# Two attentions: the heads' output brought to features by DMA, compact sums, and products of ones at the start of each

## The chip, the cores and the metric

One core of a Trainium2 chip runs the kernel. Its engines are TensorE (PE in the profile; PEld its weight loads), VectorE (DVE), ScalarE (ACT), GpSimd (POOL) and SyncE (SP, which here issues every DMA). The metric is the device time of one execution in microseconds (us), taken as the median of several.

## What is computed

Two sequences of 1024 tokens with 512 features go through six steps. Each step takes a layer norm of x and adds its result to x.

```python
x = x + 0.5 * ffn(layernorm(x))             # W + lora_B @ lora_A, scaled by column
x = x + attention0(layernorm(x))            # 32 query heads of 16, 8 key heads, rotary
x = x + 0.5 * ffn(layernorm(x))
x = x + 0.5 * experts(layernorm(x))         # base + top 2 of 8 experts of rank 16
x = x + attention1(layernorm(x))            # 8 heads of 32, scale 1
x = x + 0.5 * experts(layernorm(x))
# attention: softmax(q @ k.T * scale, causal) @ v, heads side by side, @ w_o.T + b_o
```

All of it is held to float32 accuracy. So a matrix product is made of three passes (high x high, high x low, low x high), with operands split into a high and a low part.

## The kernel before

Each sequence b runs three chains of dense stages and, between them, two attentions: chain 0 (`FFN_A`, `QKV0`), attention `QKV0`, chain 1 (`WO0`, `FFN_B`, `MOE_A`, `QKV1`), attention `QKV1`, chain 2 (`WO1`, `MOE_B`). A dense stage works on eight tiles of 128 tokens, one in each tick of its chain. In a tick TensorE transposes ("turns") the tile of one stage (`turn_x`), ScalarE casts it to its high part (`copy_turned`), VectorE takes the low part (`turned_lo`), and TensorE multiplies the tile turned a tick earlier (`product`). VectorE adds the product to x (`epilogue`), GpSimd adds biases (`bias_x`, L1484) and takes the low parts of the next stage's weights (`split_chunk`, L1466) behind ScalarE's casts of them.

An attention runs in units: 8 units of 4 heads in the first (`A0`), 4 units of 2 heads in the second (`A1`). A unit has 12 steps (c, j): c is the half of the 1024 queries, j the block of 128 keys. Steps 0 to 3 belong to half 0, steps 4 to 11 to half 1; in steps 0 to 3 and 8 to 11 the block lies on the diagonal. In each step TensorE makes the scores transposed, keys by queries (L977, L983), ScalarE takes their exponentials (L1431), GpSimd masks those on the diagonal (L1542), and two or three steps later TensorE multiplies by the values (L999). The values carry a column of ones, so the sum of the exponentials comes out as one more row of each head. Scores, exponentials and values have banks 0 to 3 and 6 of PSUM.

The exponentials need a shift, minus the maximum of each query's scores, which enters the scores as two more rows of the queries. These maxima are worked out about one unit ahead, in a ring of three PSUM banks. `plan_ring` writes the order of the ring's items out beforehand, at three slots in each step, and TensorE (`ring_item`) and VectorE (`ring_read`) both walk through it. There are three kinds of items:

- "max": TensorE makes scores in the other orientation (L871) and VectorE takes maxima by row (L1204 on the diagonal, L1208 off it).
- "shift": a half's shifts (from L1247 to L1253) are transposed (L876), copied (L1217), and SyncE writes them into the query rows by small DMAs (`load_shifts`, L606).
- "norm": when the values of half c of a unit are complete, ScalarE copies them out of PSUM (`heads_raw`, L1418). Four transposes (L881) bring them to tokens by features, VectorE takes the reciprocals of the sums (L1227) and multiplies (L1232) into `features`.

An item takes its bank when the item three places ahead has been read. The ring runs ahead of the scores from the start: the first items stand in chain 0 or 1, among the products of `QKV0` or `QKV1`, the next (`ring_first`) by themselves, and in the first steps of unit 0 more of them stand in each slot than later (`wanted`). At the end of an attention, `WO0` or `WO1` turns the eight tiles of `features` as any other stage does.

SyncE's queue holds all DMAs in one order, with waits between them. In the first attention each unit has the shifts of the next unit, the queries of the unit three ahead, and in two units a stage's weights.

## Time and profile before

| | us |
|---|---|
| median of 3 runs | 1364.15 (1360.6 to 1367.84) |
| profiled execution | 1344.81 |
| its span, first to last instruction | 1343.1 |
| TensorE busy | 1205.7 (90%) |
| VectorE busy | 953.5 (71%) |
| ScalarE busy | 671.2 (50%) |
| GpSimd busy | 375.2 (28%) |

The page gives busy time by engine, the span in 40 slices of 33.6 us, the DMA queues, the chain of waits that ended last, and groups of instructions by line. In the slices each digit is a share in tenths. The clock that TensorE was granted is given in the same way, 9 being nine tenths or more of full speed. The two sequences take about half of the span each. The attentions lie at about 108 to 358, 527 to 619, 771 to 1021 and 1186 to 1278 us.

### The profile page before, as it was taken

The numbers are of one execution on the slowest core, as the hardware profiler recorded it, in microseconds if no ns is written. First come the engines' busy times: TensorE is split into PE (matmuls) and PEld (weight loads), VectorE is DVE, ScalarE is ACT, GpSimd is POOL, SyncE is SP. The second block draws the span as 40 slices with busy tenths as digits, with TensorE's granted clock in tenths as the row PEclk, the third lists the DMA queues.
The fourth block names the chain that finished last, engine by engine and source line by source line (L and its number), as shares of the span: only waits on it lengthen the run. The fifth ranks groups of instructions, "written<-read, shape, count | busy, mean of one in ns | idle before, by whom it ended". The sixth has DMA issues, their size and how long they took to land.

```text
span 1343.1 us, 21792 instructions
## 1 busy us (share of the span) xinstructions
PE 1205.7 (90%) x6800; PEld 753.2 (56%) x6800; DVE 953.5 (71%) x2990; ACT 671.2 (50%) x1023; POOL 375.2 (28%) x505
## 2 busy tenths in 40 slices
PE   4998999999899877998879999999988988879988
PEld 1875444443388865444868744444435887744368
DVE  5889889898166676653659798999962667576365
ACT  2621666666655452544436036666665554435542
POOL 0431411122254400114614323122213542002162
PEclk9996899999999997999979858999999999869999
DMA  8374411220010020100140742112200100120001
GB/s 317 120 196 87 125 29 26 57 65 3 1 49 1 1 47 19 55 2 0 63 175 23 189 130 70 26 26 57 66 2 0 50 1 17 32 72 2 1 8 56
DMA packets 37285, 76.20 MB, mean 57 GB/s; under 512 B 5084, under 2 KB 6620, under 8 KB 37036
## 3 DMA queue, kind: packets, MB, share of 16 engines
q1 hardware_dynamic: 37176, 74.82, 19.2%
q8 instruction: 60, 0.98, 0.3%
q14 instruction: 49, 0.40, 0.1%
HBM read 48.98 MB, written 27.08 MB: 57 GB/s over the span
## 4 chain that ended last, share of the span: by engine, by line
PE 64%; DVE 19%; issue 5%; POOL 5%; ACT 5%; DMA 1%; DVEq 0%; SPq 0%; ACTq 0%; POOLq 0%
PE bank L999 16%; PE bank L871 12%; PE bank L779 5%; PE bank L780 5%; PE bank L781 5%; DVE maxes L1208 5%; PE bank L983 4%; PE bank L977 3%; DVE unused L1204 3%; PE bank L765 3%; DVE ops L1152 3%; PE bank L881 2%; POOL x L1484 2%; POOL w_odd L1466 2%; ACT ops L1356 2%
## 5 line engine op out<-in xcount | busy, mean ns | idle before, releaser
L1431 ACT ACTIVATE probs<-bank 128x1024 f32<-128x1024 f32 (+3 forms) x416 | 367.9, 911 | 320.4 <-PE bank L983 220.3
L871 PE MATMUL bank<-ops 48*128 48x512 f32 (+3 forms) x960 | 321.8, 436 | 34.5 <-DVE maxes L1204 17.2
L1204 DVE CUSTOM_DVE_ANT_0 unused<-bank,causal 128x128 bf16<-128x128 f32 (+3 forms) x640 | 279.5, 486 | 47.7 <-PE bank L871 44.1
L1542 POOL TENSOR_SCALAR_AFFINE_SELECT probs<-probs 128x256 f32<-128x256 f32 (+1 forms) x256 | 118.8, 464 | 640.3 <-ACT probs L1431 640.0
L871 PEld LDWEIGHTS bank<-ops 48*128 48x128 f32 (+1 forms) x960 | 163.0, 206 | 218.9 <-DVE maxes L1204 96.0
L999 PE MATMUL bank<-probs,v_mem 128*17 128x512 f32 (+6 forms) x1920 | 252.2, 517 | 6.1 <-ACT heads_raw L1418 5.6
L1208 DVE TENSOR_REDUCE maxes<-bank 128x1 f32<-128x512 f32 x320 | 207.4, 684 | 40.7 <-PE bank L871 39.2
L983 PE MATMUL bank<-ops 50*128 50x512 f32 (+2 forms) x640 | 175.9, 448 | 5.0 <-ACT probs L1431 4.8
L779 PE MATMUL bank<-ops,xT 128*128 128x512 f32 (+1 forms) x288 | 116.2, 403 | 19.6 <-DVE x L1068 11.6
L983 PEld LDWEIGHTS bank<-ops 50*128 50x128 f32 x640 | 86.6, 197 | 57.9 <-ACT probs L1431 29.5
L1473 POOL TENSOR_TENSOR rstd<-var_eps,minus_half 128x1 f32<-128x1 f32 x96 | 52.7, 549 | 215.1 <-DVE var_eps L1046 214.5
L1315 ACT CAST xT<-bank 128x512 fp32r<-128x512 f32 (+1 forms) x96 | 52.6, 548 | 118.0 <-PE bank L765 117.9
L1055 DVE TENSOR_TENSOR xT<-bank,xT 128x512 fp32r<-128x512 f32 (+1 forms) x96 | 61.5, 643 | 67.5 <-ACT xT L1315 67.1
L780 PE MATMUL bank<-ops,xT 128*128 128x512 f32 (+1 forms) x288 | 105.5, 366 | 0.0
L781 PE MATMUL bank<-ops,xT 128*128 128x512 f32 (+1 forms) x288 | 105.5, 366 | 0.0
L999 PEld LDWEIGHTS bank<-probs,v_mem 128*17 128x17 f32 (+1 forms) x1920 | 40.9, 99 | 77.1 <-issue 52.0
L1374 ACT ACTIVATE probs<-x,ln_bias,rstd 128x512 f32<-128x512 f32 x96 | 78.3, 816 | 3.2
L779 PE MATMUL bank<-w_odd,xT 128*128 128x324 f32 (+1 forms) x192 | 72.8, 379 | 5.8 <-DVE x L1068 2.7
L1227 DVE RECIPROCAL inv_sum<-bank 128x16 f32<-128x16 f32 (+1 forms) x48 | 11.3, 234 | 92.6 <-PE bank L881 92.6
L779 PEld LDWEIGHTS bank<-ops,xT 128*128 128x128 f32 x288 | 56.4, 196 | 31.2 <-issue 21.4
L765 PE MATMUL bank<-identf,probs 128*128 128x128 f32 x384 | 57.8, 280 | 16.0 <-ACT probs L1374 16.0
L1042 DVE BATCH_NORM_STATS2 stats<-x 128x6 f32<-128x512 f32 x96 | 65.8, 686 | 3.7 <-DMA x<-x_dram 3.3
(117 smaller groups left out, 1965.5 us busy)
## 6 DMA issues: line engine op xcount, KB each, us to landing
query_rows_dram<-ops SPq DMA_DIRECT2D x48, 256.0 KB, 3.8
ops<-query_rows_dram SPq DMA_DIRECT2D x64, 192.0 KB, 4.4
w_odd<-staging_wqkv SPq DMA_DIRECT2D x4, 1536.0 KB, 7.3
x<-x_dram SPq DMA_DIRECT2D x16, 256.0 KB, 6.1
ops<-ops SPq DMA_DIRECT2D x16, 256.0 KB, 3.0
out_dram<-x SPq DMA_DIRECT2D x16, 256.0 KB, 2.0
staging_wqkv<-wqkv_dram SPq DMA_DIRECT2D x2, 1536.0 KB, 15.8
key_rows_dram<-ops SPq DMA_DIRECT2D x24, 128.0 KB
```

The source lines that it names most:

```text
L765: last = nc.tensor.transpose(turn[n % 2][:, k * P:(k + 1) * P], src[:, k * P:(k + 1) * P], identf[:])
L779: mm(dst, x_hi[:, k, :], hi[:, k, :], start=(k == 0), stop=False)
L780: mm(dst, x_hi[:, k, :], lo[:, k, :], start=False, stop=False)
L781: last = mm(dst, x_lo[:, k, :], hi[:, k, :], start=False, stop=(k == kc - 1 and not lora))
L871: last = mm(dst[:, h * w:(h + 1) * w], queries(a, u)[rows, t // 4, hi, t % 4 * P:(t % 4 + 1) * P], keys(a, u, hi)[rows, HALF * kp:HALF * k ...
L983: last = mm(dst, keys(a, u, 0)[rows, block], queries(a, u)[rows, c, heads_of[0]:heads_of[-1] + 1, columns], start=True, stop=True)
L999: last = mm(heads[a.head_rows * h:a.head_rows * h + a.dim + 1, q0 - HALF * c:HALF], v[:, j, a.kv_head(u, r, i), :], probs[:, e % 6, n, fir ...
L1204: V.tensor_tensor_reduce(unused[:, masked % 3, 0:w], part, causal[:, HALF - w:], 1.0, NEG, ALU.add, ALU.max, dst).then_inc(s["max_done"].s ...
L1208: V.tensor_reduce(dst, part, AX.X, ALU.max).then_inc(s["max_done"].sem, 1)
L1374: A.activation(xn[n % XN_SLOTS], x[:, t, :], ACT.Identity, bias=ln_bias[:, i, :], scale=rstd[:, i, :]).then_inc(xn_ready.sem, 1)
L1431: A.activation(probs[:, e % 6, :, 0:cols], scores[:, 2 * (e % 2):2 * (e % 2) + 2, 0:cols], ACT.Exp, scale=a.scale).then_inc(s["exp"].sem, 1)
L1542: G.affine_select(out=p, in_=p, compare_op=ALU.is_ge, fill=0.0, base=0, pattern=pattern, channel_multiplier=-1).then_inc(s["masked"].sem, 1)
```

## The change

The "norm" items leave the ring, and with them the transposes L881, the reciprocals L1227 and the multiplications L1232. `heads_raw` keeps the heads as rows and queries as columns, and this is also what the output product wants of its operand, features by tokens. So the change never turns them:

- SyncE writes a chunk of `heads_raw` to DRAM (`load_heads`). It reads the heads' rows back, packed into 64 partitions for a unit, and the rows of sums as 128 partitions of 16 (8 in the second attention).
- For each pair of units and half, VectorE takes the reciprocals of the compact sums (`inverse_sums`). SyncE stores them and loads them back spread over the rows of each head (`spread_inverse`).
- GpSimd multiplies, casts to the high part and subtracts for the low part (`heads_out`), ahead of step 4 of a later unit. For the last pair VectorE does this (`last_heads`), half 0 at the end of the attention, half 1 in tick 5 of the chain that follows.
- `WO0` and `WO1` take these parts (`heads_T`) as their operands. Their turns, ScalarE's copies of them and VectorE's low parts are gone. The products of tiles 0 to 3 wait for half 0, those of tiles 4 to 7 for half 1.
- ScalarE's copy of a chunk waits for the dump of the chunk two back, where it waited for a ring item.
- The parts lie where `MOE_A`'s weights were loaded early. These weights are now loaded after `WO0` and split at tiles 4 to 7 of `FFN_B`, not 2 to 5. `xT` has moved to the end of `ops`.
- TensorE multiplies a 128x128 block of ones by a 128x512 one, in bfloat16, ahead of every second "max" item between the chain's part of the ring and step 3 of the first unit. The result goes to the item's own bank, which the item then overwrites. There are 20 of these in each first attention and 7 in each second.

```diff
-                if slot == 0:
-                    for c in range(2):
-                        e = s - self.lag - 2 - self.last_step[c]
-                        if e >= 0 and e % ns == 0 and e // ns < self.units:
-                            dst.append(("norm", e // ns, c))
         self.ring = self.ring_first + [x for step in self.ring_at for slot in step for x in slot]
         self.ring_len = len(self.ring)
-        self.norm_at = [i for i, item in enumerate(self.ring) if item[0] == "norm"]
...
+        def heads_T(a, part, k):
+            first = ((4096, 5120, 6144, 7168), (8192, 9216, 21504, 14336)) if a is A0 else ((1024, 3072), (4096, 5120))
+            return ops_flat[:, first[part][k]:first[part][k] + SEQ]
...
+            def load_heads(b, st, u, c):
+                a, s = ATT[st], qs[st]
+                lanes, n = slice(64 * (u % 2), 64 * (u % 2) + 64), a.unit_heads * HALF // P
+                sp.wait_ge(s["raw"].sem, s["raw"].at(b, 2 * u + c + 1))
+                wait(sp, s["staged"][c], b, 32 * u)
+                sp.dma_start(raw_rows[c], heads_raw[:, c, :]).then_inc(s["dumped"][c].sem, 16)
+                sp.wait_ge(s["dumped"][c].sem, s["dumped"][c].at(b, 16 * (u + 1)))
+                if u == 0 and c == 0 and a.rope:
+                    sp.wait_ge(s["lo"].sem, s["lo"].at(b, 6))
+                if u > 3:
+                    sp.wait_ge(s["out"].sem, s["out"].at(b, 3 * (2 * (u // 2 - 2) + c) + 1))
+                rows = raw_rows[c].rearrange("(h r) s -> h r s", r=a.head_rows)
+                sp.dma_start(head_in[lanes, u // 2 % 2, c, :], rows[:, 0:a.dim, :]).then_inc(s["staged"][c].sem, 16)
+                sp.dma_start(sums[:, c, u % 2, 0:n], rows[:, a.dim, :].rearrange("h (l x) -> h l x", x=n)
+                             ).then_inc(s["staged"][c].sem, 16)
+            def spread_inverse(b, st, k, c):
+                a, s = ATT[st], qs[st]
+                n = a.unit_heads * HALF // P
+                flat = inverse_rows[c, 0:2 * n * P]
+                sp.wait_ge(s["inverse"].sem, s["inverse"].at(b, 2 * k + c + 1))
+                wait(sp, s["spread"][c], b, 16 * k)
+                sp.dma_start(flat.rearrange("(u l x) -> l u x", u=2, x=n), sums[:, c, :, 0:n]).then_inc(s["inverse_stored"].sem, 16)
+                sp.wait_ge(s["inverse_stored"].sem, s["inverse_stored"].at(b, 16 * (2 * k + c + 1)))
+                if k > 0:
+                    sp.wait_ge(s["out"].sem, s["out"].at(b, 3 * (2 * (k - 1) + c) + 1))
+                rows = flat.rearrange("(h s) -> h s", s=HALF).unsqueeze(1)
+                sp.dma_start(head_inv[:, c, :], rows.to_broadcast([2 * a.unit_heads, a.dim, HALF])).then_inc(s["spread"][c].sem, 16)
...
+                    if u % 2 == 0 and u > 0:
+                        spread_inverse(b, QKV0, u // 2 - 1, 1)
+                    load_heads(b, QKV0, u, 0)
+                    if u % 2:
+                        spread_inverse(b, QKV0, u // 2, 0)
+                    if u + 1 < a.units:
                         load_shifts(b, QKV0, u + 1, 1)
                     if u + 3 < a.units:
 
                         sp.wait_ge(s["scored"].sem, s["scored"].at(b, (u + 1) * a.unit_events))
                         load_queries(b, u + 3, 0)
                         load_queries(b, u + 3, 1)
-                    if u in (3, 4):
-                        load_weights(b, FFN_B if u == 3 else MOE_A)
+                    if u == 3:
+                        load_weights(b, FFN_B)
+                    load_heads(b, QKV0, u, 1)
+                spread_inverse(b, QKV0, a.units // 2 - 1, 1)
...
+                load_weights(b, MOE_A)
...
                 n = product_no(st, t)
-                pe.wait_ge(xT_ready.sem, xT_ready.at(b, TURN_NO[st, t] + 1))
+                if st in WO_ATT:
+                    a, s = WO_ATT[st], qs[QKV0 if st == WO0 else QKV1]
+                    pe.wait_ge(s["out"].sem, s["out"].at(b, 3 * (a.units - 2)))
+                    pe.wait_ge(s["last"].sem, s["last"].at(b, 3 * (t // 4 + 1)))
+                else:
+                    pe.wait_ge(xT_ready.sem, xT_ready.at(b, TURN_NO[st, t] + 1))
                 wait(pe, x_new, b, n - 1)
...
                     operands_ready(b, st, u, t)
+                    if max(a.begun.values()) <= i < len(a.ring_first) + sum(len(slot) for step in a.ring_at[:3] for slot in step) and i % 2:
+                        mm(dst, ones_b[:, 0:P], ones_b[:, :], start=True, stop=True)
...
-                else:
-                    c = 2 * u + n
-                    pe.wait_ge(s["raw"].sem, s["raw"].at(b, c + 1))
-                    for j in range(4):
-                        last = nc.tensor.transpose(dst[:, j * P:(j + 1) * P],
-                                                   heads_raw[:, c % 2, j * P:(j + 1) * P], identf[:])
...
+                    if c > 0 and i == 3:
+                        inverse_sums(b, QKV0 if c == 1 else QKV1, (A0 if c == 1 else A1).units // 2 - 1, 1)
+                    if c > 0 and i == 5:
+                        last_heads(b, QKV0 if c == 1 else QKV1, 1)
...
-                    V.reciprocal(inv_sum[:, 0:4 * nh].unsqueeze(2), blocks[:, :, d:d + 1]).then_inc(s["inv"].sem, 1)
-                    dve.wait_ge(s["inv"].sem, s["inv"].at(b, c + 1))
-                    width = a.q_feats
-                    dst = features[:, :].rearrange("p (t f) -> p t f", f=D)[
-                        :, 4 * n:4 * n + 4, u * nh * d:(u + 1) * nh * d].rearrange("p t (h d) -> p t h d", h=nh)
-                    V.tensor_tensor(dst, src.rearrange("p (t h r) -> p t h r", t=4, h=nh)[:, :, :, 0:d],
-                                    inv_sum[:, 0:4 * nh].rearrange("p (t h) -> p t h", t=4).unsqueeze(3)
-                                    .to_broadcast([P, 4, nh, d]), ALU.mult).then_inc(s["normed"].sem, 1)
+            def inverse_sums(b, st, k, c):
+                a, s = ATT[st], qs[st]
+                part = sums[:, c, :, 0:a.unit_heads * HALF // P]
+                dve.wait_ge(s["staged"][c].sem, s["staged"][c].at(b, 32 * (2 * k + 2)))
+                V.reciprocal(part, part).then_inc(s["inverse"].sem, 1)
+            def last_heads(b, st, c):
+                a, s = ATT[st], qs[st]
+                k = a.units // 2 - 1
+                hi, lo = (heads_T(a, part, k)[:, HALF * c:HALF * (c + 1)] for part in range(2))
+                dve.wait_ge(s["spread"][c].sem, s["spread"][c].at(b, 16 * (k + 1)))
+                dve.wait_ge(s["out"].sem, s["out"].at(b, 3 * (2 * (k - 1) + c + 1)))
+                V.tensor_tensor(head_out[:, c, :], head_in[:, k % 2, c, :], head_inv[:, c, :], ALU.mult).then_inc(s["last"].sem, 1)
+                dve.wait_ge(s["last"].sem, s["last"].at(b, 3 * c + 1))
+                V.tensor_copy(hi, head_out[:, c, :]).then_inc(s["last"].sem, 1)
+                dve.wait_ge(s["last"].sem, s["last"].at(b, 3 * c + 2))
+                V.tensor_tensor(lo, head_out[:, c, :], hi.bitcast(F32), ALU.subtract).then_inc(s["last"].sem, 1)
 
             def attention(b, st):
-                for i in range(max(ATT[st].begun.values()), ATT[st].ring_len):
-                    ring_read(b, st, i)
+                a = ATT[st]
+                ring_no = max(a.begun.values())
+                for g, step in [(-1, [a.ring_first])] + list(enumerate(a.ring_at)):
+                    upto = len(a.ring_first) + sum(len(slot) for before in a.ring_at[:g + 1] for slot in before)
+                    for i in range(ring_no, upto):
+                        ring_read(b, st, i)
+                    ring_no = upto
+                    u, k_ = divmod(g, len(a.steps))
+                    if u % 2 == 0 and 0 < u < a.units and k_ == 6:
+                        inverse_sums(b, st, u // 2 - 1, 1)
+                    if u % 2 == 1 and u < a.units and k_ == 10:
+                        inverse_sums(b, st, u // 2, 0)
+                last_heads(b, st, 0)
...
-                                act.wait_ge(s["ring_full"].sem, s["ring_full"].at(b, a.norm_at[ch - 2] + 1))
+                                act.wait_ge(s["dumped"][c].sem, s["dumped"][c].at(b, 16 * (ch // 2)))
...
+                        first = 4 if nst == MOE_A else 2
+                        if nb < BATCH and nst not in WO_ATT and first <= t < first + chunks_of[nst]:
+                            split_chunk(nb, nst, t - first)
...
+            def heads_out(b, st, k, c):
+                a, s = ATT[st], qs[st]
+                n = 3 * (2 * k + c)
+                hi, lo = (heads_T(a, part, k)[:, HALF * c:HALF * (c + 1)] for part in range(2))
+                pool.wait_ge(s["staged"][c].sem, s["staged"][c].at(b, 32 * (2 * k + 2)))
+                pool.wait_ge(s["spread"][c].sem, s["spread"][c].at(b, 16 * (k + 1)))
+                G.tensor_tensor(head_out[:, c, :], head_in[:, k % 2, c, :], head_inv[:, c, :], ALU.mult).then_inc(s["out"].sem, 1)
+                pool.wait_ge(s["out"].sem, s["out"].at(b, n + 1))
+                G.tensor_copy(hi, head_out[:, c, :]).then_inc(s["out"].sem, 1)
+                pool.wait_ge(s["out"].sem, s["out"].at(b, n + 2))
+                G.tensor_tensor(lo, head_out[:, c, :], hi.bitcast(F32), ALU.subtract).then_inc(s["out"].sem, 1)
...
+                    if u > 1 and k_ == 4:
+                        heads_out(b, st, u // 2 - 1, u % 2)
```

SyncE's queue in the first attention, around units 1 to 3. `shiftT` are the shifts, `query_rows` the queries. Before:

```order
45 L606 DMA ops<-shiftT 1x8x128 x8
46 L639 DMA ops<-query_rows_dram 48x2x512 x4
47 L606 DMA ops<-shiftT 1x8x128 x8
48 L639 DMA ops<-query_rows_dram 48x2x512 x4
49 L606 DMA ops<-shiftT 1x8x128 x8
50 L639 DMA ops<-query_rows_dram 48x2x512 x4
```

With the change, from the queries of one unit to those of the next but one (`raw_rows` holds a dumped chunk, `inverse_rows` the inverses):

```order
61 L674 DMA ops<-query_rows_dram 48x2x512 x4
62 L619 DMA raw_rows_dram<-heads_raw 128x512
63 L626 DMA features<-raw_rows_dram 64x1x512
64 L627 DMA sums<-raw_rows_dram 128x1x16
65 L609 DMA ops<-shiftT 1x8x128 x4
66 L637 DMA inverse_rows_dram<-sums 128x2x16
67 L642 DMA features<-inverse_rows_dram 128x1x512
68 L619 DMA raw_rows_dram<-heads_raw 128x512
69 L626 DMA features<-raw_rows_dram 64x1x512
70 L627 DMA sums<-raw_rows_dram 128x1x16
71 L609 DMA ops<-shiftT 1x8x128 x4
72 L674 DMA ops<-query_rows_dram 48x2x512 x4
```

The second half's four shift loads stand behind a dump, its two loads, a store and a spreading load.

TensorE at the start of the first attention, behind the last product of `QKV0`. Before:

```order
292 L871 MATMUL bank<-ops 128x512 x3
293 L876 MATMUL bank<-identf,shifts 32x128
294 L871 MATMUL bank<-ops 128x512
295 L871 MATMUL bank<-ops 128x128 x4
296 L871 MATMUL bank<-ops 128x512 x4
297 L871 MATMUL bank<-ops 128x256 x4
298 L871 MATMUL bank<-ops 128x512 x3
299 L983 MATMUL bank<-ops 128x512 x2
```

With the change (L928 is the product of ones, L931 the maxima, L936 the shifts):

```order
292 L931 MATMUL bank<-ops 128x512
293 L928 MATMUL bank<-ones_b 128x512
294 L931 MATMUL bank<-ops 128x512 x2
295 L936 MATMUL bank<-identf,shifts 32x128
296 L931 MATMUL bank<-ops 128x512
297 L928 MATMUL bank<-ones_b 128x512
298 L931 MATMUL bank<-ops 128x128 x4
299 L928 MATMUL bank<-ones_b 128x512
300 L931 MATMUL bank<-ops 128x512 x2
301 L928 MATMUL bank<-ones_b 128x512
302 L931 MATMUL bank<-ops 128x512 x2
303 L928 MATMUL bank<-ones_b 128x512
```

Between the maxima stand seven products of ones ahead of the first scores, and thirteen more behind.

GpSimd in the first attention, masks only. Before:

```order
75 L1542 AFFINE_SELECT probs<-probs 128x2x128 x4
76 L1542 AFFINE_SELECT probs<-probs 128x4x128
77 L1542 AFFINE_SELECT probs<-probs 128x2x256
78 L1542 AFFINE_SELECT probs<-probs 128x2x128 x4
79 L1542 AFFINE_SELECT probs<-probs 128x4x128
```

With the change (L1633 are the masks):

```order
85 L1633 AFFINE_SELECT probs<-probs 128x4x128
86 L1633 AFFINE_SELECT probs<-probs 128x2x256
87 L1605 TENSOR_TENSOR features<-features 128x512
88 L1607 CAST ops<-features 128x512
89 L1609 TENSOR_TENSOR ops<-features,ops 128x512
90 L1633 AFFINE_SELECT probs<-probs 128x2x128 x4
91 L1633 AFFINE_SELECT probs<-probs 128x4x128
```

Three operations on 128x512 elements have come between the masks of steps 3 and 8.

## Rows read from the trace of the kernel before

**Rows 1.** The page: busy time of each engine; TensorE's granted clock by slice.

```profile
PE 1205.7 (90%) x6800; PEld 753.2 (56%) x6800; DVE 953.5 (71%) x2990; ACT 671.2 (50%) x1023; POOL 375.2 (28%) x505
...
PEclk9996899999999997999979858999999999869999
```

**Rows 2.** Busy time by stretch: two units of the first attention, its last the second.

```profile
core 0: us, PE busy (x) PEld busy (x) DVE busy (x) ACT busy (x) POOL busy (x), PEclk, DMA share, GB/s
...
202.30:230.60 28.30, 27.55 (x197) 11.73 (x194) 26.32 (x92) 19.02 (x24) 5.80 (x12) 1.00 0.14 30
...
317.80:346.20 28.40, 22.84 (x168) 8.49 (x165) 14.55 (x42) 18.54 (x24) 5.80 (x12) 1.00 0.01 2
```

**Rows 3.** Chain of waits by line: two units of either attention, first the first's.

```profile
by line: PE bank L999 31.3%; PE bank L871 28.5%; DVE maxes L1208 13.3%; PE bank L983 11.7%; issue 5.1%; DVE unused L1204 4.5%; PE bank L881 4.2%; DVE maxes L1204 1.6%; PE bank L876 0.7%; DVEq L1202 0.1%
...
by line: PE bank L999 41.8%; PE bank L871 24.9%; PE bank L977 23.6%; PE bank L881 4.0%; ACT heads_raw L1418 2.7%; ACT probs L1431 1.4%; PE bank L876 1.0%; issue 0.7%
```

**Rows 4.** Groups of instructions by line: busy, mean ns of one, idle before.

```profile
L881 PE MATMUL bank<-identf,heads_raw 128*128 128x128 f32 x192 | 31.5, 288 | 5.5 <-ACT heads_raw L1418 3.1 <-DVE maxes L1208 2.3
L1484 POOL TENSOR_TENSOR x<-x,bo 128x512 f32<-128x512 f32 x32 | 41.0, 1286 | 0.0
...
L1232 DVE TENSOR_TENSOR features<-bank,inv_sum 128x256 f32<-128x256 f32 x48 | 20.4, 424 | 1.7
...
L1227 DVE RECIPROCAL inv_sum<-bank 128x16 f32<-128x16 f32 (+1 forms) x48 | 11.3, 234 | 92.6 <-PE bank L881 92.6
```

**Rows 5.** Timeline (start, length, instruction, idle before it): GpSimd, and VectorE beside it.

```profile
210.59 0.41 POOL L1542 TENSOR_SCALAR_AFFINE_SELECT probs<-probs 128x256 f32<-128x256 f32 x1 [13.58 <-ACT probs L1431]
...
134.61 2.35 POOL L1497 TENSOR_TENSOR ops<-features,ops 128x1024 fp32r<-128x1024 f32 x1
134.71 2.29 DVE L1253 SCALAR_TENSOR_TENSOR shifts<-maxes,shifts 128x16 fp32r<-128x16 f32 x1
```

**Rows 6.** Timeline: one unit's second shift rows, and the scores that want them.

```profile
188.49 0.18 DVE L1253 SCALAR_TENSOR_TENSOR shifts<-maxes,shifts 128x16 fp32r<-128x16 f32 x1
...
190.45 2.63 SPq L606 DMA_DIRECT2D ops<-shiftT  x4
...
197.18 0.50 PE L983 MATMUL bank<-ops 50*128 50x512 f32 x2
```

**Rows 7.** DMA issues (count, size, us to landing); timeline: VectorE's wait for a load.

```profile
out_dram<-x SPq DMA_DIRECT2D x16, 256.0 KB, 2.0
...
689.54 0.69 DVE L1042 BATCH_NORM_STATS2 stats<-x 128x6 f32<-128x512 f32 x1 [3.27 <-DMA x<-x_dram]
```

**Rows 8.** Timeline: from the first attention into its output product, first sequence.

```profile
346.12 0.62 ACT L1418 COPY heads_raw<-bank 128x512 f32<-128x512 f32 x1
...
362.10 0.71 PE L779 MATMUL bank<-w_odd,xT 128*128 128x512 f32 x1 [0.96 <-DVE xT L1055]
...
386.14 0.48 PE L779 MATMUL bank<-w_odd,xT 128*128 128x512 f32 x1
...
388.77 0.39 PE L781 MATMUL bank<-w_odd,xT 128*128 128x512 f32 x1
```

**Rows 9.** Timeline: from the second attention into its output product, first sequence.

```profile
609.01 0.58 ACT L1418 COPY heads_raw<-bank 128x512 f32<-128x512 f32 x1
...
621.99 0.79 PE L779 MATMUL bank<-ops,xT 128*128 128x512 f32 x1 [0.70 <-DVE xT L1055]
...
626.38 1.59 POOL L1466 TENSOR_TENSOR w_odd<-w_odd 128x648 fp32r<-128x648 f32 x1 [6.83 <-ACT w_odd L1324]
...
640.22 0.39 PE L781 MATMUL bank<-ops,xT 128*128 128x512 f32 x1
```

**Rows 10.** Busy time by stretch: starts of three attentions (columns as in rows 2).

```profile
112.00:148.00 36.00, 34.11 (x127) 17.33 (x126) 31.48 (x103) 13.59 (x15) 7.58 (x8) 0.53 0.59 163
764.00:816.00 52.00, 49.13 (x187) 27.20 (x187) 43.38 (x138) 15.64 (x17) 10.09 (x10) 0.51 0.42 116
528.00:540.00 12.00, 11.83 (x33) 6.89 (x33) 8.98 (x35) 3.84 (x5) 1.63 (x4) 0.51 0.30 96
```

116 lines of the change are left out of this document (62 added, 54 removed).

## The prediction

> **What bounds the kernel now.** I read the page's busy shares and clock line first, then the two attentions unit by unit, then the chain of waits. TensorE is busy for 90% of the span at a mean clock that falls in a few slices [rows 1]; the low slices are those in which an attention starts. In steady units of the first attention (28.3 us each) TensorE is busy 27.55 us and VectorE 26.32 us, both near the full length [rows 2]. The chain of waits passes back and forth between TensorE's products and VectorE's maxima, and the transposes of the heads (L881) hold 4.2% of it there, 4.0% in the second attention [rows 3]. Work that leaves both engines therefore shortens a unit. In the last unit (row 317.80) VectorE is down to 14.55 us and TensorE to 22.84: the exponentials set the pace, and the same work taken out gains nothing.
>
> **The change, part by part.** The sum is made against the profiled execution's own 1344.81 us and then scaled to the median, 1364.15; the two lie 1.4% apart.
>
> *The transposes of the heads leave the ring.* 48 groups of four go, with 48 reciprocals (0.23 us) and 48 multiplications (0.42 us) on VectorE [rows 4]. In the first attention the chain gives L881 4.2% of 57.7 us, so 2.4 us for four groups, 0.60 each. VectorE loses 0.65 us a group and gets back one reciprocal per two chunks, so it does not become the new bound. 13 groups per sequence lie before the tail: 13 x 0.60 x 2 = 15.6 us. In the second, 4.0% of 43.8 us is 1.75 us for four groups, 0.44 each; 5.5 groups per sequence lie before its tail: 4.8 us. Ends: half of this if VectorE's order keeps TensorE waiting anyway, all of it and 2 us more if the waits around the groups go too.
>
> *GpSimd gets three operations of 128x512 for each pair of units and half.* The nearest row is the bias addition, 1.29 us [rows 4], so up to 3.9 us in a unit. They stand ahead of steps 4 to 7, in which GpSimd has nothing to mask: it sits idle for 13.58 us there [rows 5]. Cost zero, hidden in that gap; beyond 13 us they would delay the masks and with them the values. One collision is possible: a VectorE operation with two inputs in SBUF took 2.29 us in place of 0.18 while GpSimd ran a 2.35 us one [rows 5]. The Trainium skill (SBUF — State Buffer, "SBUF: two separate sides") says that VectorE with two SBUF inputs and GpSimd take a shared pair of ports as an exclusive lock for a whole instruction; the trace agrees. The maxima read PSUM and at most one SBUF input; the two-input operations of a half come just ahead of step 4 and at the end of the unit, so I take nothing for it in the sum and keep it as a rival.
>
> *SyncE's queue.* Per chunk it now issues a dump, waits for it, issues two loads; per pair a store of the inverses, a wait, and a spreading load. The load of the second half's shift rows stands behind that in odd units, and TensorE's scores of step 4 wait for these rows. Before: last maximum worked up at 188.49, four shift loads issued 190.45 to 193.08, wanted at 197.18 [rows 6]. After: the reciprocal runs two short maxima later, about 189.5; store landed 191.8 (2.2 us, between a 256 KB store's 2.0 and a load's 3.27 [rows 7]); the spreading load issued by 192.4; shift loads by 195.1, landed 2 us later at 197.1. So no slack is left: 0 to 2 us late in each of six such places, I take 0.5: +3 us. In the second attention only two loads are issued and the store is over earlier; nothing.
>
> *The turn to the output product.* Before, the last chunk is transposed, divided, transposed again, cast and split ahead of the first product. After, the operand's parts come by the DMA chain. Its price: three large transfers at 2.7 us (2.0 to 3.27), a small one at 2.2, a second issue 0.6 (2.63 us for four [rows 6]), the reciprocal 0.25, three VectorE operations of 512 columns at 0.7, handoffs 0.6: 13.9 us, ends 11 and 17. First attention: the first half's chunk is copied at 346.12 to 346.74, so its parts are ready at 360.6 and the product starts at 360.8, where it was 362.10 [rows 8]. The tiles also lose their transposes; a product's matmuls stand 0.24 us apart (eleven gaps from 386.14 to 388.77), and eight tiles from 362.10 to 389.0 hold seven turns of 0.35: 2.5 us. The second half's chain starts its reciprocal behind the first tile's update (about 365.9) and ends at 373.5, when tile 3 ends: no wait. End 385.2 for 389.0: -3.8 us, twice -7.6. Ends: 0 and -5 each.
>
> Second attention: copied by 609.59, ready at 623.5, where the product started at 621.99 [rows 9]. Its tiles are half as long: first tile done 626.4, update 627.1, then 7.7 us for reciprocal, store, spreading and split: 634.8. Four tiles of six matmuls and the next stage's turns end at 641.3, later if the clock fell in the wait. Before: 640.5. GpSimd no longer holds this stretch: it had waited 6.83 us for a cast that stood behind the turned tile's copy (626.38), and that copy is gone, so it is ahead from now on. I take +1.5 us, twice +3. Ends -2 and +5 each.
>
> *Weights of the expert stage* load after the output product and are split two tiles later, a stage ahead of their use: zero.
>
> *The ones products.* 20 in each first attention, 7 in each second. At full clock one costs 0.24 us, at half clock 0.48. In the starts of the attentions the granted clock is 0.53, 0.51 and 0.51, about the 1.2 GHz level, and VectorE idles 4.5, 8.6 and 3.0 us in them [rows 10]; at the steady share (2.0 of 28.3) it would be 2.5, 3.6 and 0.8. If the products keep the clock at 2.4 GHz, the gain is 2.0 + 5.0 + 2.2 + 2.2 (the second sequence's like the first's) = 11 us. If they don't, 13 of 20 stand among scores and are paid at 0.48, and all 7: 2 x (6.2 + 3.4) = 19 us. What speaks for: the products use all rows and TensorE sits waiting for VectorE here. Against: during 112 to 148 TensorE was busy 34.11 of 36 us and the clock still stayed low. Between these ends I take 0. The Trainium skill (TensorE: Matmul & The Clock Gate, "What's actually happening") states that the throttled clock is the default and activity releases it; by that alone the first end would hold, and the sum would be 11 us lower. The row of 112 to 148 does not fit it without more.
>
> **Sum.** -15.6 - 4.8 + 3 - 7.6 + 3 + 0 = -22 us: 1322.8 for 1344.81, a factor 0.9836, and 1342 us for the median.
>
> **The rivals.**
> 1. The clock holds through the starts: 11 us more, 1331. For it: idle TensorE rows at the start of an attention; against: the busy stretch above. 0.20.
> 2. The clock does not hold (that part does not do what it says) and the products are paid: +19, 1361. 0.14.
> 3. The shared ports: one two-input VectorE operation per unit falls into a GpSimd one and loses 0.9 us (between 0 and 1.29) in the units with such work: 16 x 0.9 = +14, 1356. Against it is the order of the operations. 0.05.
> 4. Slower: the transfers of the sums and inverses in pieces of 64 bytes (32 in the second attention) land late. Each chunk's sums and each pair's inverses go so. At d us more for each, six shift waits grow by d, the turns by about 2d (four of them, of which the later ones twice). At d = 3: 6 x 3 + 2 x 6 + 2 x 6 = 42, so +20 against the old kernel, scaled 1384. It decides from d = 1.6 on, where the gain is gone. The shift rows, 512 bytes a piece, land in about 2 us, which speaks against it. The Trainium skill (DMA: Bandwidth & Descriptors, "Why small descriptors are slow") says that small pieces are slow for HBM; no run here shows these sizes, and the amount is only 8 to 16 KB. 0.09.
>
> **How the numbers follow.** The forecast, 1334 to 1350, has 0.52. Faster than before by over 0.5% (about what a measurement can tell, so below 1357.3) hold the forecast, rival 1, and parts of 2 and 3: 0.78. Within 0.5%: the rest of 2 and 3 and the mild end of 4, 0.13. Slower: 0.09. The range 1325 to 1362 takes in the forecast, most of rival 1, rivals 2 and 3, and leaves rival 4 and the far end of 1 out.
>
> **What would show it.** Units of the first attention of 27.1 us in place of 28.3; no wait of the scores for shift rows above 1 us; the first output product at about 361 and 623.5 less what was gained ahead of it; GpSimd's three operations ended ahead of the masks of step 8; the granted clock in the four starts near 1.0 (rival 1) or still 0.5 with fewer idle VectorE microseconds (rival 2). The prediction is wrong if units keep 28 us although L881 is gone, or if the turns take over 17 us from the copy.

## The result, and the profile after

The change makes the kernel slower. Its median is 1374.65 us (1368.35 to 1378.83, 6 runs) against 1362.33 for the kernel before (1356.39 to 1367.84, 6 runs): a ratio of 1.0104, with an interval of 1.0059 to 1.0149. On another chip the same pair gave 1.0118 (1.0065 to 1.0172, `change_again` below). The ratios, here and below, leave out executions more than 1.5% above the fastest of the same kernel. I had forecast 1342 us, a ratio of 0.984.

The profiled execution of the change has a span of 1366.3 us, that of the kernel before 1343.1. The profiled one of before was short: 1344.81 us, below all six timed runs. So the two traces differ by 23 us where the medians differ by 12, and I read pieces from them, not the total.

First the page of the change: the busy times, and TensorE's granted clock by slice. Against [rows 1] TensorE has 11.6 us less work and VectorE 16 us less, although 27.1 us of products of ones came in, and yet the span is longer. Work was taken out; waiting came in. The mean granted clock of the span is lower too, 0.910 for 0.928.

```profile
PE 1194.1 (87%) x6560; PEld 728.6 (53%) x6566; DVE 937.5 (69%) x2911; ACT 655.9 (48%) x991; POOL 427.8 (31%) x553
...
PEclk8996799799999998997989958899999999989889
```

**At full clock the units did what they were to do.** Busy time by stretch: two units of the first attention with the change, of which [rows 2] show the one before.

```profile
core 0: us, PE busy (x) PEld busy (x) DVE busy (x) ACT busy (x) POOL busy (x), PEclk, DMA share, GB/s
198.28:225.36 27.08, 26.38 (x188) 10.78 (x188) 25.30 (x89) 18.86 (x23) 8.93 (x15) 1.00 0.31 73
252.83:285.28 32.45, 31.95 (x188) 13.12 (x190) 25.66 (x89) 19.09 (x22) 8.91 (x15) 0.75 0.34 94
```

The first unit takes 27.08 us where it took 28.30, and VectorE 25.30 where it was busy for 26.32. The second takes 32.45 us with the same number of matmuls, because the clock was at 0.75 of full speed. One such fall costs 5 us, four units' gain. They come in the kernel before as well, at other places and of other lengths: from the first copy of the heads to the first half's last one its first attentions have a mean clock of 0.97 and 0.97, those of the change 0.94 and 0.92. What brings them no run here separates.

**The turn to the output product is where most of the time went.** (Turn is here the passage from an attention to its output product, not a transpose.) The timeline around the second attention's last copies, first sequence: SyncE, then VectorE, then TensorE (start, length, instruction, idle before it and its cause). The rows of the kernel before are [rows 9].

```profile
609.48 0.33 SPq L619 DMA_DIRECT2D raw_rows_dram<-heads_raw  x1
611.86 0.51 SPq L626 DMA_DIRECT2D features<-raw_rows_dram  x1
612.41 0.48 SPq L627 DMA_DIRECT2D sums<-raw_rows_dram  x1
617.80 0.37 SPq L637 DMA_DIRECT2D inverse_rows_dram<-sums  x1
619.37 0.56 SPq L642 DMA_DIRECT2D features<-inverse_rows_dram  x1
...
617.52 0.25 DVE L1282 RECIPROCAL sums<-sums 128x16 f32<-128x16 f32 x1 [20.22 <-DMA sums<-raw_rows_dram]
624.89 1.99 DVE L1291 TENSOR_TENSOR features<-features 128x512 f32<-128x512 f32 x1 [7.12 <-DMA features<-inverse_rows_dram]
626.92 1.37 DVE L1293 CAST ops<-features 128x512 fp32r<-128x512 f32 x1
628.32 0.69 DVE L1295 TENSOR_TENSOR ops<-features,ops 128x512 fp32r<-128x512 f32 x1
...
629.12 0.77 PE L830 MATMUL bank<-ops 128*128 128x512 f32 x1 [11.22 <-issue]
...
641.72 0.77 PE L830 MATMUL bank<-ops 128*128 128x512 f32 x1 [4.39 <-issue]
```

The copy of the first half starts at 608.88. The dump is issued at 609.48 and has landed when the loads are issued, at 611.86. Then nothing happens on VectorE until 617.52: the reciprocal waits for both loads. The spreading load, issued at 619.37, lands at 624.89. VectorE's three operations take 1.99, 1.37 and 0.69 us. TensorE starts at 629.12, after 11.22 us of idling: 20.2 us behind the copy's start, where it was 13.0 in the kernel before. At tile 4 it idles once more, 4.39 us at 641.72, for the second half's chain.

The same stretch by busy time, with the clock and the share of the 16 DMA engines:

```profile
618.60:624.60 6.00, 0.00 (x0) 0.00 (x0) 0.00 (x0) 2.56 (x5) 5.64 (x5) 0.68 0.27 84
624.60:629.10 4.50, 0.00 (x0) 0.01 (x1) 4.05 (x3) 0.00 (x0) 3.40 (x3) 0.50 0.08 20
629.10:634.10 5.00, 4.99 (x12) 3.94 (x13) 0.85 (x2) 0.00 (x0) 0.00 (x0) 0.50 0.08 17
```

In the wait the clock has fallen, to a mean of 0.68 and then 0.50, and the product's first 5 us are paid at 0.50. The first attention's turn is less bad: 18.5 us from copy to product for 16.0 before, and tile 4 doesn't wait.

**The products of ones were paid.** Timeline of TensorE near the start of the first attention, first sequence, and their group over the whole execution (busy, mean ns, idle before):

```profile
113.25 0.39 PE L928 MATMUL bank<-ones_b 128*128 128x512 bf16 x1
...
120.98 0.61 PE L928 MATMUL bank<-ones_b 128*128 128x512 bf16 x1
...
L928 PE MATMUL bank<-ones_b 128*128 128x512 bf16 x48 | 27.1, 564 | 8.7 <-DVE maxes L1266 8.5
...
124.00:136.00 12.00, 11.53 (x34) 5.39 (x34) 10.41 (x41) 1.62 (x2) 0.98 (x3) 0.50 0.13 24
```

They last 0.61 us each once the clock is down, and it comes down as it did without them: over 124 to 136 us the granted clock is 0.50. The first copy of the heads stands at 150.72 us, in the kernel before at 143.24. Of the 54, the weight loads show all and the matmul records 48, so the 27.1 us are those of 48.

**Minor terms.** Scores waited for shift rows seldom, 0.6 us in all in the first attentions and 6.8 us in six places of the second (kernel before: 0.8). GpSimd's three operations waited 0.5 us for their data and lie in the gap they were put in.

```profile
PEld bank L1030 <- DMA ops<-shiftT: 6.8, 6, 2.0
...
PEld bank L1036 <- DMA ops<-shiftT: 0.6, 1, 0.6
```

### The profile page after: what moved, and what is told of

It is laid out like the page before. It is cut to its first block, busy times and chain, and to the rows that moved or that the text cites. A ratio compares the mean times of both kernels' runs of the same rounds, so it can differ in the third digit from the quotient of the medians.

```text
span 1366.3 us, 21474 instructions
## 1 busy us (share of the span) xinstructions
PE 1194.1 (87%) x6560; PEld 728.6 (53%) x6566; DVE 937.5 (69%) x2911; ACT 655.9 (48%) x991; POOL 427.8 (31%) x553
## 4 chain that ended last, share of the span: by engine, by line
PE 63%; DVE 17%; issue 7%; ACT 5%; POOL 4%; DMA 3%; SPq 1%; DVEq 0%; ACTq 0%; POOLq 0%
PE bank L1052 14%; PE bank L931 13%; PE bank L830 6%; PE bank L831 5%; PE bank L832 5%; PE bank L1036 4%; DVE maxes L1266 4%; PE bank L1030 3%; DVE ops L1206 3%; DVE unused L1262 2%; PE bank L813 2%; ACT ops L1430 2%; POOL x L1559 2%; PE bank L928 2%; PE bank L855 1%
## 5 line engine op out<-in xcount | busy, mean ns | idle before, releaser
L931 PE MATMUL bank<-ops 48*128 48x512 f32 (+3 forms) x960 | 322.9, 444 | 33.7 <-DVE maxes L1262 19.0
L1633 POOL TENSOR_SCALAR_AFFINE_SELECT probs<-probs 128x256 f32<-128x256 f32 (+1 forms) x256 | 118.8, 464 | 590.9 <-ACT probs L1506 590.9
L931 PEld LDWEIGHTS bank<-ops 48*128 48x128 f32 (+1 forms) x960 | 161.2, 209 | 222.5 <-DVE maxes L1262 100.7
L1052 PE MATMUL bank<-probs,v_mem 128*17 128x512 f32 (+6 forms) x1920 | 255.6, 525 | 6.1 <-ACT heads_raw L1493 5.6
L1036 PE MATMUL bank<-ops 50*128 50x512 f32 (+2 forms) x640 | 182.6, 457 | 5.2 <-ACT probs L1506 5.0
L830 PE MATMUL bank<-ops 128*128 128x512 f32 (+1 forms) x288 | 117.6, 408 | 44.4 <-issue 31.1
L1036 PEld LDWEIGHTS bank<-ops 50*128 50x128 f32 x640 | 92.6, 205 | 58.2 <-issue 27.8
L831 PE MATMUL bank<-ops 128*128 128x512 f32 (+1 forms) x288 | 107.1, 372 | 0.0
L832 PE MATMUL bank<-ops 128*128 128x512 f32 (+1 forms) x288 | 107.1, 372 | 0.0
L1389 ACT CAST ops<-bank 128x512 fp32r<-128x512 f32 x96 | 55.2, 584 | 102.3 <-PE bank L813 102.1
L1109 DVE TENSOR_TENSOR ops<-bank,ops 128x512 fp32r<-128x512 f32 x96 | 65.1, 686 | 36.9 <-ACT ops L1389 36.6
L830 PE MATMUL bank<-w_odd,ops 128*128 128x324 f32 (+1 forms) x192 | 73.2, 381 | 16.7 <-POOL ops L1541 7.1
L830 PEld LDWEIGHTS bank<-ops 128*128 128x128 f32 x288 | 57.7, 200 | 55.7 <-issue 46.1
L1441 ACT ACTIVATE ln_bias<-minus_mean,rstd 128x1 f32<-128x1 f32 x96 | 28.2, 294 | 122.4 <-POOL rstd L1548 121.8
```

What stands on the lines that cost most here:

```text
L830: mm(dst, x_hi[k], hi[:, k, :], start=(k == 0), stop=False)
L831: mm(dst, x_hi[k], lo[:, k, :], start=False, stop=False)
L832: last = mm(dst, x_lo[k], hi[:, k, :], start=False, stop=(k == kc - 1 and not lora))
L931: last = mm(dst[:, h * w:(h + 1) * w], queries(a, u)[rows, t // 4, hi, t % 4 * P:(t % 4 + 1) * P], keys(a, u, hi)[rows, HALF * kp:HALF * k ...
L1036: last = mm(dst, keys(a, u, 0)[rows, block], queries(a, u)[rows, c, heads_of[0]:heads_of[-1] + 1, columns], start=True, stop=True)
L1052: last = mm(heads[a.head_rows * h:a.head_rows * h + a.dim + 1, q0 - HALF * c:HALF], v[:, j, a.kv_head(u, r, i), :], probs[:, e % 6, n, fir ...
```

## The experiments

Each ratio is to the kernel before, run on the same chip, with its 95% interval. From the third experiment on the base isn't always the change itself; each says what it stands on. The first four kernels below ran on one chip, the next four on a second, the next four on a third, and the last four on the second again, so a step from one group to the next goes over two chips and has both intervals. The turn is given throughout as the time from the start of the first half's last copy to the start of the first output product, read from TensorE's and ScalarE's timelines: 16.0 us (first attention) and 13.0 us (second) in the kernel before, 17.3 to 18.5 and 20.2 in the change.

### Without the products of ones, and with nothing but them

```diff
-                    if max(a.begun.values()) <= i < len(a.ring_first) + ... and i % 2:
-                        mm(dst, ones_b[:, 0:P], ones_b[:, :], start=True, stop=True)
```

> The changed kernel without its 54 products of ones, all else the same. In its trace they stand mostly at half clock (0.61 us each in the rows, about 0.43 us apart when back to back) in stretches in which TensorE is busy for 97% or more. Theory P (they are paid): 27 per sequence, of which about 22 at half clock, give 22 x 0.43 + 5 x 0.24 = 10.7 us less per sequence if nothing hides them, 8 if the idle of TensorE takes in some: 16 to 21 us in all, 1354 to 1359 for the median of 1374.65, so this part alone would turn the change from a gain of some 5 us to the loss of 12. Theory T (the loss is in the turns to the output products): the products cost at most 4 us in all, 1371 to 1375. Rival H (they held the clock for part of the starts): without them the time grows. In the first sequence the first copy of the heads stood at 150.72 with them and at 143.24 in the kernel before; P expects 143 to 145 here.

Measured: 1.003 (0.9988 to 1.0073) for 1.0104, so 10 us less, though the two intervals overlap. The first copy stands at 143.57 us. The second kernel is the kernel before with these lines added:

> The kernel before with nothing but the products of ones, ahead of every second maximum item from the end of the chain's part of the ring to step 3 of the first unit, as in the changed kernel. Theory P: 16 to 21 us slower than before (1378 to 1383 against 1362), with the granted clock at the starts still at half. Theory H: faster by up to 11 us with the clock near full in the starts. If they are paid by TensorE's idle time alone, 0 to +4.

Measured: 1.007 (1.0035 to 1.0106), 9.5 us more. Its stretch at the first start (columns as above):

```profile
112.00:149.00 37.00, 36.51 (x127) 14.98 (x127) 28.77 (x98) 10.80 (x12) 7.46 (x8) 0.53 0.47 123
```

The clock is 0.53 there, as in [rows 10], with 36.51 of 37 us busy. So the products cost 10 us whichever kernel they stand in, and hold no clock. Theory P had the mechanism, with a price too high (16 to 21). TensorE waits 8.7 us for a maximum just before some of them (the group's row), so part of them may fall into idle time; that this is the difference isn't shown. The rest of the change gains nothing by itself: 1.003 isn't 0.984.

### The chain of transfers without its second half

```diff
-                    if u % 2:
+                    if u % 2 and u < a.units - 1:
                         spread_inverse(b, QKV0, u // 2, 0)
...
-                dve.wait_ge(s["spread"][c].sem, s["spread"][c].at(b, 16 * (k + 1)))
+                dve.wait_ge(s["staged"][c].sem, s["staged"][c].at(b, 32 * (2 * k + 2)))
+                dve.wait_ge(s["spread"][c].sem, s["spread"][c].at(b, 16 * k))
```

> The changed kernel, in which the last pair of units of each attention is multiplied by the inverses of the pair before: the division of the last pair by its own sums is left out, with the reciprocal, its store and the spreading load of that pair; the dump, the loads of heads and of sums stay. This takes sums, reciprocal, store and spreading load from between the last copy and the output product: by the trace of the changed kernel from 354.0 to 363.0 in the first attention and from 612.9 to 624.9 in the second, of which the landing of the loads (some 2 us) stays. Theory T: 7 us less per first attention and 9 to 10 us less per second, and in the second attention a clock that does not fall in the wait gives 2 to 4 us more: 32 to 42 us in all, 1333 to 1343. Rival G (GpSimd's biases and splits or the second half's chain are late next and hold the product): under 12 us, 1363 to 1370.

Measured: 0.9806 (0.9756 to 0.9856), 40 us less than the change, the upper end of theory T. The turns come to 11.4 and 12.9 us, and the wait at tile 4 of the second attention to 1.26 for 4.39: 17.6 us in the first sequence, and so about 35 of the 40 in both. Even with the products of ones in it, this kernel is where I had forecast the whole change. So the loss is in this chain, which ends at TensorE's first output product and at its tile 4.

### Three ways to shorten it that failed

A wide reciprocal, with the sums loaded spread:

```diff
+                if u >= a.units - 2:
+                    sp.wait_ge(s["out"].sem, s["out"].at(b, 3 * (2 * (a.units // 2 - 2) + c) + 1))
+                    sp.dma_start(head_inv[lanes, c, :], rows[:, a.dim, :].unsqueeze(1).to_broadcast(
+                        [a.unit_heads, a.dim, HALF])).then_inc(s["staged"][c].sem, 16)
+                    return
...
+                V.reciprocal(head_inv[:, c, :], head_inv[:, c, :]).then_inc(s["inverse"].sem, 1)
```

> The changed kernel, in which for the last pair of units the row of sums of each head is loaded already spread over its rows (one 2 KB piece for each of the 128 rows, from the dumped chunk, beside the heads), and VectorE takes the reciprocal of all 128x512 of them, in place of compact sums, a small reciprocal, a store and a spreading load. All results are computed. From the reciprocals' 0.24 us for 16 and 0.34 for 32 columns the wide one should take 3.3 us. Theory T: the chain loses the compact load (3.2 and 5.1 us from issue to landing), the store (1.6) and the spreading load (3.8 and 5.5) and gets a load of 3 to 4 us and 3.3 us on VectorE: 3 us less per first attention and 6 to 7 less per second, with the clock 2 more: 20 to 24 us in all, 1350 to 1355. Rival G: no more than 6 us.

Measured: 1.0205 (1.0155 to 1.0255), slower than the change. The reciprocal took 3.35 us as worked out, but the first sequence's turns stayed at 18.4 and 20.0 us. In the second attention the two loads of two heads each, issued at 632.40, land 7.96 us later, at 640.36, where the heads' and the compact load took 5.66. With the wide reciprocal the multiplication starts 15.8 us behind the copy, where it was 16.0 by way of the store and the spreading load. VectorE does the same for the second half behind the first tiles' updates, and tile 4 of the first attentions, which had not waited, waits 3.3 us in each. That is 6.6 of the 14 us over the change; the rest I can't place. The profiled run, the slowest of the four at 1387.07 us, had its last unit of the first attention at a clock of 0.59, but the other three lie above the change as well.

The sums straight from SBUF, ahead of the dump:

```diff
+                sp.dma_start(sums[:, c, u % 2, 0:n], heads_raw[a.dim::a.head_rows, c, :].rearrange("h (l x) -> h l x", x=n)
+                             ).then_inc(s["staged"][c].sem, 16)
                 sp.dma_start(raw_rows[c], heads_raw[:, c, :]).then_inc(s["dumped"][c].sem, 16)
```

> The changed kernel without the products of ones, with the row of sums loaded into its compact form straight from the copied heads in SBUF, ahead of the dump, where it was loaded from the dump. The dump and the heads' load stay, beside reciprocal and store. Base: the kernel without the products of ones, 1.003 of before. Theory T (every step of the chain from the last copy to the output product is paid in full): the dump, 2.4 us in the second attention and 3.8 in the first, leaves the chain: 2 x (2.4 + 3.8) = 12 us less, ratio 0.994. Rival G (next is something else, such as the load of the heads, which now comes later): 0 to 4 us, ratio 1.000 to 1.003. Rival Q (the compact load from SBUF is slower than from DRAM or holds the dump back): no gain or a loss, above 1.003.

Measured: 1.0049 (1.0012 to 1.0086) for 1.003: nothing gained, rival G. Its timeline of the second attention's turn:

```profile
605.96 0.52 SPq L621 DMA_DIRECT2D sums<-heads_raw  x1
...
609.19 0.52 SPq L630 DMA_DIRECT2D features<-raw_rows_dram  x1
...
614.66 0.25 DVE L1282 RECIPROCAL sums<-sums 128x16 f32<-128x16 f32 x1 [20.87 <-DMA features<-raw_rows_dram]
```

The sums are now asked for 0.6 us behind the copy's start, where it was 3.5, and the reciprocal starts at 614.66 all the same, 8.7 us behind that. It waits for both loads on one semaphore, and the heads' load, issued at 609.19, is the late one. So the suspect is the 128 KB load and not the small pieces.

Pieces of 256 bytes for the sums:

```diff
-        sums = sb("sums", [P, 2, 2, 16])
+        sums = sb("sums", [32, 2, 2, 64])
```

> The changed kernel without the products of ones, with the compact sums as 32 or 16 rows of 64 elements (256 bytes a piece) in place of 128 rows of 16 or 8 (64 or 32 bytes). Theory B (the pieces' number and size set the compact load's 3.2 us in the first and 5.1 us in the second attention and the store's 1.6): the load comes to 2 to 2.5 us, 1 us less per first and 2.5 per second attention, against 0.4 to 0.5 us more for the reciprocal of 128 columns: 2 to 6 us less in all, ratio 0.999 to 1.001. Rival F (a transfer's latency is fixed, or set by the heads' load issued ahead of it): nothing gained, ratio 1.003 to 1.004.

Measured: 1.0241 (1.02 to 1.0283), 28 us slower than its base. As rival F had it, the loads didn't get faster (5.53 us from issue to reciprocal in the second attention). The turns are 17.3 and 20.0 us, unchanged. The reciprocal of 128 columns takes 0.94 us for 0.34 (0.24 in the second attention), 24 times, 15 us more for VectorE, which is near the bound in the first attention; the mean clock of its runs is 0.883 to 0.891, where the runs of its base had 0.897 to 0.921. So pieces of 32 and 64 bytes were not what made the loads late. Why it lost more than the 15 us the trace doesn't say.

The early biases, on the change without the products of ones (a first edit here that isn't about the transfers):

```diff
                     for st, t in tick.turns:
...
-                        bias_x(b, st, t)
+                        if st not in WO_ATT:
+                            bias_x(b, st, t)
...
+                    if k_ in (5, 6) and u >= 1 and g < (a.units - 1) * ns:
+                        for t in [t for t in range(NT) if a is A0 and k_ == 5 and t in ((u - 1,) if u < 6 else (5, 6, 7))] + \
+                                [t for t in range(NT) if a is A1 and t // 2 == 2 * (u - 1) + (k_ - 5)]:
+                            bias_x(b, st + 1, t)
```

> The changed kernel without the products of ones, in which GpSimd adds the output products' biases to x inside the attentions, at steps 5 and 6 of their units, where it was idle, and no longer at the turn, beside VectorE's three operations on the last heads. In the changed kernel these took 0.69 + 1.37 + 1.63 us in the first attention and 1.99 + 1.37 + 0.69 in the second for the first half, against 0.69 + 0.43 + 0.69 for the second half. Theory S (shared ports): up to 2 us less per turn, 8 us in all, ratio 0.997 to 0.999, and the three operations at 1.8 us; GpSimd's splits of the next weights, which stay, can keep part of it. Rival: the units lose by the additions what the turns gain (a VectorE operation with two inputs from SBUF beside them): ratio 1.003 or above.

Measured: 0.9969 (0.9932 to 1.0005) for 1.003, 8 us less, with overlapping intervals. The three operations in the second attention's turn take 0.69, 0.43 and 0.69 us, and the turns are 16.5 and 17.9 us. Theory S holds there. In the first attention's turn of the same trace they still take 0.69, 1.38 and 1.63 us: GpSimd splits the next stage's weights from 364.36 on, and the cast starts at 364.54. A fourth kernel had direct sums, pieces of 256 bytes and early biases together:

> The three edits together, without the products of ones: sums straight from SBUF, biases early, pieces of 256 bytes. Theory T: they add up, 12 + 8 + 4 = 24 us less than 1.003, ratio 0.985, and the output products start 12 to 14 us behind the copy of the first half, where it was 18 and 19.7. If the second half's chain or the clock's fall in the wait hold instead, the ratio stays above 0.995.

Measured: 1.0155 (1.0112 to 1.0199), 12 us less than the pieces of 256 bytes alone, and above 0.995 as the expectation's alternative had it. The pieces' loss hides the biases' gain.

### The heads' load, and how many DMA engines it has

In the change the DMA share in the heads' load of the second attention is 0.12 to 0.14, two of 16 engines, and the load's pattern is two heads by 32 rows. Two edits follow from that: let nothing wait for this load that needn't, and issue a DMA for each head.

```diff
+                sp.dma_start(sums[:, c, u % 2, 0:n], heads_raw[a.dim::a.head_rows, c, :].rearrange("h (l x) -> h l x", x=n)
+                             ).then_inc(s["dumped"][c].sem, 16)
                 sp.dma_start(raw_rows[c], heads_raw[:, c, :]).then_inc(s["dumped"][c].sem, 16)
...
-                dve.wait_ge(s["staged"][c].sem, s["staged"][c].at(b, 32 * (2 * k + 2)))
+                dve.wait_ge(s["dumped"][c].sem, s["dumped"][c].at(b, 32 * (2 * k + 2)))
                 V.reciprocal(part, part).then_inc(s["inverse"].sem, 1)
```

> Biases early, no products of ones, and the compact sums loaded straight from SBUF beside the dump, with the reciprocal waiting for these two and no longer for the load of the heads, which then runs beside reciprocal, store and spreading load. Base: the kernel with early biases and no products of ones, 0.997 of before. In the run with direct sums the reciprocal still waited for the heads' load, 609.19 to 614.66 in the second attention, and gained nothing. Theory E (the heads' load is the long step: it goes over as many of the 16 DMA engines as the piece has heads, four in the first and two in the second attention, as the DMA shares of 0.21 and 0.13 in its time show): without it in the chain each first attention's turn is 2 to 3.5 us shorter and each second's 4 to 5, with the second half's chain as well: 12 to 17 us in all, ratio 0.984 to 0.988. Rival V (the chain's end is set by something else next, as in the run with direct sums): 0.995 to 0.999.

GpSimd's `heads_out` and `last_heads` now wait for the heads' load by its own count.

Measured: 0.9897 (0.9858 to 0.9936) for 0.9969, between the two expectations and nearer to theory E. The turns come to 13.8 and 16.9 us. The first attention's is 2.7 us shorter, as expected; the second's only 1.0, where 4 to 5 were expected. SyncE's rows there say why:

```profile
592.95 0.52 SPq L630 DMA_DIRECT2D features<-raw_rows_dram  x1
593.57 0.38 SPq L639 DMA_DIRECT2D inverse_rows_dram<-sums  x1
598.44 0.56 SPq L644 DMA_DIRECT2D features<-inverse_rows_dram  x1
```

The reciprocal starts at 592.96, 3.8 us behind the copy, so it is off the heads' load. But the 8 KB store of the inverses, issued 0.6 us behind that load, has landed only at 598.44, 4.87 us later, where the change's took 1.57: not before the load of 128 KB ahead of it, which took 5.5 us with direct sums. So the heads' load left the reciprocal's wait and stayed in the chain, by way of the transfer issued behind it. The same is seen in the change itself: the second half's dump, issued at 620.02 behind the spreading load, takes 5.42 us, the first half's 2.38.

```diff
+                    for h in range(a.unit_heads):
+                        at = lanes.start + a.dim * h
+                        sp.dma_start(head_in[at:at + a.dim, u // 2 % 2, c, :], rows[h, 0:a.dim, :]).then_inc(s["staged"][c].sem, 16)
...
+                    for h in range(2 * a.unit_heads):
+                        sp.dma_start(head_inv[a.dim * h:a.dim * (h + 1), c, :], rows[h, 0].partition_broadcast(a.dim)
+                                     ).then_inc(s["spread"][c].sem, 16)
```

> Biases early, no products of ones, and in the second attention one DMA for each head, for the heads' loads (2 of 32 rows in place of 1 of 64) and for the spreading loads (4 of 32 rows in place of 1 of 128). Theory E (a transfer's outermost dimension sets how many DMA engines share it): the DMA share in the heads' load goes from 0.13 to 0.5 or more and the load lands in 3 us in place of 5, the spreading load in 4 in place of 5.5, both with their further issues on SyncE: 3 to 4 us less per second attention and half, 5 to 8 us in all, ratio 0.991 to 0.994. Rival L (the loads' time is a fixed latency, and the share is low because the amounts are small): two more issues of 0.55 us each and nothing gained, ratio 0.997 to 1.000.

Measured: 0.989 (0.9827 to 0.9953) for 0.9969, somewhat more than theory E's range; the turn of the second attention is 16.3 us for 17.9. Busy time by stretch in the change, one microsecond each, in the heads' load of the second attention (columns as before):

```profile
613.90:614.90 1.00, 1.00 (x6) 0.31 (x6) 0.00 (x0) 0.59 (x1) 0.27 (x1) 1.00 0.12 41
...
615.90:616.90 1.00, 1.00 (x8) 0.35 (x6) 0.00 (x0) 0.14 (x1) 0.79 (x2) 1.00 0.14 41
```

and in the same load with one DMA for each head:

```profile
616.10:617.10 1.00, 1.00 (x8) 0.41 (x6) 0.00 (x0) 0.49 (x2) 0.41 (x1) 1.00 0.56 129
```

About the same 128 KB move in one microsecond with a share of 0.56, where they took three at 0.12 to 0.14. On SyncE, VectorE and GpSimd of this kernel:

```profile
615.31 0.77 SPq L629 DMA_DIRECT2D features<-raw_rows_dram  x2
616.12 0.54 SPq L632 DMA_DIRECT2D sums<-raw_rows_dram  x1
...
618.22 0.25 DVE L1290 RECIPROCAL sums<-sums 128x16 f32<-128x16 f32 x1 [17.08 <-DMA sums<-raw_rows_dram]
623.48 1.80 DVE L1299 TENSOR_TENSOR features<-features 128x512 f32<-128x512 f32 x1 [5.01 <-DMA features<-inverse_rows_dram]
625.32 1.65 DVE L1301 CAST ops<-features 128x512 fp32r<-128x512 f32 x1
627.00 1.92 DVE L1303 TENSOR_TENSOR ops<-features,ops 128x512 fp32r<-128x512 f32 x1
...
623.17 5.20 POOL L1549 TENSOR_TENSOR w_odd<-w_odd 128x648 fp32r<-128x648 f32 x3 [2.83 <-ACT w_odd L1406]
```

From the first load's issue to the reciprocal it is 2.91 us, where the change has 5.66 (611.86 to 617.52). The transfers together bring the multiplication 5.1 us nearer to the copy (10.8 us behind it, where its base has 15.9), and the turn shows only 1.5 of them: the three operations now fall beside GpSimd's splits and take 5.4 us in place of 1.8, although the biases are early. And the first attention's transfers without the products of ones, with four heads in the heads' load (first row) and eight in the spreading load:

```profile
349.20:350.20 1.00, 1.00 (x8) 0.37 (x4) 0.00 (x0) 0.79 (x2) 0.00 (x0) 1.00 0.21 80
...
354.90:355.90 1.00, 1.00 (x14) 0.37 (x18) 0.00 (x0) 0.63 (x2) 0.67 (x2) 1.00 0.49 188
```

Shares of 0.21 and 0.49: close to four and eight of 16. Theory E holds, and rival L, a fixed latency, doesn't.

> Both edits together (sums beside the dump with the reciprocal not waiting for the heads, and one DMA for each head in the second attention), biases early, no products of ones. Theory E: the heads' load is off the chain already, so of the second edit only the spreading load's 1.5 us counts: 3 us less than the first alone, ratio 0.982 to 0.986. If either edit's gain was of another origin they do not meet so: 0.99 or above.

Measured: 0.9655 (0.9593 to 0.9717), more than the two gains added (1.5%) and more than theory E expected, whose premise, that the heads' load was off the chain already, was wrong. The turns are 13.5 and 11.1 to 12.7 us. The trace shows two things that each edit alone had lost: the store of the inverses takes 1.65 us again (597.60 to 599.25) behind the short heads' loads, and in the first sequence the three operations take 1.8 us, since GpSimd's splits begin only beside the last of them. On another chip the same kernel was at 0.9705; see below.

### Products of ones where TensorE does idle

```diff
+                    if t == 0:
+                        wait(pe, x_new, b, n - 1)
+                        for _ in range(24 if st == WO0 else 44):
+                            mm(prod[n % 2][:, 0, :], ones_b[:, 0:P], ones_b[:, :], start=True, stop=True)
```

> Biases early, no products of ones in the attentions, but 24 of them ahead of the first tile of the first output product and 44 ahead of the first tile of the second, in the time in which TensorE waited (7 and 11 us) for the last heads. Theory C (the wait lets the clock fall, and it is paid in the tiles behind it: the granted clock was 0.50 for the first 5 us of either output product): with TensorE kept busy the clock stays at full there, 2 to 2.5 us less per turn, 8 to 10 in all, ratio 0.989 to 0.992. Rival N (the clock falls all the same, as it did in the starts of the attentions with TensorE busy): no gain, 0.997, or a loss of up to 8 us where the products end later than the heads are ready.

Measured: 0.9962 (0.9919 to 1.0004) for 0.9969: no gain that these intervals show. Busy time by stretch in its first sequence's second turn, and tile 4 behind it:

```profile
611.00:618.00 7.00, 7.00 (x40) 3.19 (x35) 0.25 (x1) 3.21 (x6) 4.59 (x3) 1.00 0.22 68
618.00:626.00 8.00, 7.37 (x34) 4.65 (x31) 3.35 (x7) 0.00 (x0) 0.00 (x0) 1.00 0.08 24
...
634.20 0.77 PE L834 MATMUL bank<-ops 128*128 128x512 f32 x1 [6.47 <-issue]
```

Here the clock did stay at 1.00. From the copy to the next stage's first product the first attentions take 40.0 and 39.7 us, where the kernel without these products (`bias_early`) takes 41.8 and 41.2: there nothing waits at tile 4, and the clock is worth 1.5 to 1.8 us, near theory C. The second attentions take 40.4 and 40.9 us for 39.7 and 39.9. There TensorE goes on to wait at tile 4 for the second half's chain, 6.47 us at 634.20 where it was 5.27, so faster tiles 0 to 3 only wait longer; behind the wait the clock is down again (the next nine products stand 0.43 us apart), and in the second sequence the products of ones ran past the moment at which the heads were ready (first output product 19.7 us behind the copy for 18.0). The four together give 1.5 us, which no median here can show. A clock kept up in a stretch is worth what no wait behind it takes back.

### The whole difference, step by step on one chip

> The changed kernel as it is, on the chip of the three others. All theories: about 1.010 of before, as before.

> The changed kernel with its products of ones and its late biases, and the two edits of the chain: compact sums straight from SBUF with the reciprocal waiting for them and the dump alone, and in the second attention one DMA for each head. Theory T (the chain at the turns is what the change loses most by): from 1.010 to 0.978 to 0.985. Rival A (the two edits gave more than their sum only because the biases were early): 0.99 to 1.00.

> As the run before it in this list, without the products of ones. Theory P: they cost 0.7% as in the kernel before and in the change, so 0.971 to 0.978. Rival H (with short turns they hold the clock): no difference, or slower without them.

> Both edits of the chain, no products of ones, early biases: 0.9655 on another chip. If biases early are worth 0.6% as on the long chain, 0.965 to 0.972. If the first result was luck of the clock: 0.975 or above.

| kernel | ratio to before | interval | turns, us |
|---|---|---|---|
| the change | 1.0118 | 1.0065 to 1.0172 | 17.3, 20.0 |
| + both edits of the chain | 0.9939 | 0.9902 to 0.9975 | 15.6, 14.1 |
| + no products of ones | 0.9854 | 0.9803 to 0.9904 | 16.0, 14.1 |
| + early biases | 0.9705 | 0.9654 to 0.9755 | 13.4, 11.2 |

The turns are the first sequence's. The two DMA edits give 1.8% (24 us), the products of ones 0.85% (11 us), as theory P had it, the early biases 1.5% (20 us), and the last kernel confirms the 0.9655 of the other chip. Of each kernel the edits are those shown above. The chain's edits alone came out at 0.9939, in rival A's range and not in theory T's (0.978 to 0.985): in that trace the three operations of the second turn take 4.9 us. The early biases shorten the four turns by 10 us in all, half of their 20; where the other half comes from the traces don't say. The timeline of the last kernel's second turn, to be laid beside the change's:

```profile
588.40 0.55 SPq L621 DMA_DIRECT2D sums<-heads_raw  x1
...
591.13 0.77 SPq L633 DMA_DIRECT2D features<-raw_rows_dram  x2
592.00 0.38 SPq L644 DMA_DIRECT2D inverse_rows_dram<-sums  x1
593.60 1.70 SPq L651 DMA_DIRECT2D features<-inverse_rows_dram  x4
...
591.14 0.25 DVE L1292 RECIPROCAL sums<-sums 128x16 f32<-128x16 f32 x1 [14.91 <-DMA raw_rows_dram<-heads_raw]
596.97 0.69 DVE L1302 TENSOR_TENSOR features<-features 128x512 f32<-128x512 f32 x1 [5.57 <-DMA features<-inverse_rows_dram]
597.69 0.43 DVE L1304 CAST ops<-features 128x512 fp32r<-128x512 f32 x1
598.15 0.69 DVE L1306 TENSOR_TENSOR ops<-features,ops 128x512 fp32r<-128x512 f32 x1
...
598.95 0.47 PE L842 MATMUL bank<-ops 128*128 128x512 f32 x1 [2.13 <-issue]
```

The reciprocal starts 3.3 us behind the copy's start (587.80) in place of 8.6, the three operations take 1.8 us for 4.05, and TensorE idles 2.13 us in place of 11.22. In the second sequence GpSimd's splits start 0.2 us before the last of the three, which then takes 1.93 us, and that turn is 12.7 us long: part of the gain hangs on when the splits fall. This kernel takes 1312.47 us (1307.41 to 1319.58) where the kernel before takes 1350.73 on that chip: 0.9705, the fastest of all here.

## Why the prediction was wrong

The two traces of the change can be cut into the same pieces as the one trace of the kernel before, and each piece set against the forecast (us, difference to the kernel before, both sequences together):

| piece | forecast | the change | `change_again` |
|---|---|---|---|
| attentions, first copy of heads to the first half's last copy | -17.4 | -6.1 | -13.3 |
| from that copy through the output product to the next stage's first product | -4.6 | +20.6 | +19.2 |
| the rest, with the starts of the attentions | 0 | +8.7 | +9.8 |
| whole span | -22 | +23.2 | +15.7 |

The second row is the largest miss. The third is about the price of the products of ones. In the first the gain came at full clock and was lost in part where the clock was lower.

**The heads' groups leave the ring: right at full clock.** I forecast units of 27.1 us; the trace has 27.08, where [rows 2] have 28.30. Of the 17.4 us in the first row 6 and 13 came: most of the rest is lost in units at a lower clock, which the sum didn't price, as the unit of 32.45 us above. With the second attention's turn near the kernel before's (14.1 us for 13.0) and without the products of ones (the third row of the table of ratios) the change comes to 0.9854, and I had forecast 0.984.

**The turn's price: the step that failed.** It was put together from "three large transfers at 2.7 us" and a small one at 2.2, 13.9 us in all, ends 11 and 17. The change has 17.3 to 18.5 us in the first attention and 20.2 in the second, counted from the copy's start (14.7 and 14.5 by the forecast): 3 and 6 us too little. Of the second's 5.7 us the heads' load and its companion have 2.4 (5.66 for 2.7 and 0.6), the spreading load 2.8 (5.52 for 2.7) and VectorE's three operations 2.0 (4.05 for 2.1), while dump, store and handoffs came out 1.4 shorter. The rows for the 2.7 us, [rows 7], are transfers of 256 KB whose pattern is 128 rows, and their 3.27 is the time for which VectorE idled, not a transfer's. The page of the kernel before had dearer ones of the same size (median us from issue to landing, some of them queued behind others), which the sum passed over:

```profile
query_rows_dram<-ops SPq DMA_DIRECT2D x48, 256.0 KB, 3.8
x<-x_dram SPq DMA_DIRECT2D x16, 256.0 KB, 6.1
```

The heads' load of the second attention has two heads outermost, got two of 16 engines and took 5.5 us (609.19 to 614.66 with direct sums) for half the bytes, the spreading load with four heads 5.5 us. The Trainium skill (DMA: Bandwidth & Descriptors, "Rules for kernel authors" and "Why a DMA increments its semaphore by 16 and not by 1") says just this: the slowest dimension that isn't 1, on both sides, sets how many of the 16 engines share a transfer, so one smaller than 16 confines it. The shares of 0.13, 0.21 and 0.49 for two, four and eight heads agree, and so does the 0.56 of the pieces of 32 rows, above what eight of 16 could have. The price is paid twice, since a transfer issued behind such a load, which has few engines, landed no earlier than it (the store in the kernel with sums beside the dump, 4.87 us for 1.57). I had read another section of that page and not laid this rule beside `load_heads` and `spread_inverse`. The turn of over 17 us was named as what would make the prediction wrong, but had no rival of its own.

**And the same again for the second half.** "When tile 3 ends: no wait" held in the first attention, but from the copy to the next stage that took 43.8 and 43.1 us where I had 39.4: the 2.5 us of transposes that went are used up by the later start and by its low clock. In the second "7.7 us for reciprocal, store, spreading and split" started at 632.66, when the late first tile was through, and took until 641.62, so tile 4 started at 641.72 after 4.39 us of idling. The next stage's products begin at 650.22 where they began at 641.63: the turn costs 8.6 us there, and I had 1.5. Each such wait brings a lower clock behind it, which the sum mentions and doesn't price.

**VectorE's operations at 0.7 us: wrong beside GpSimd.** Rival 3 took the ports' collision for the units, where it doesn't appear (the two-input operations of the shifts take 0.43 and 0.20 us on average, before 0.45 and 0.28), and gave it 0.05. It stood in the turn, where GpSimd adds biases and splits weights without pause: 4.05 us for 1.8. The early biases show it in the second attention; with the biases gone the splits alone do the same when they fall beside it (5.4 us in `per_head`). The Trainium skill ("SBUF: two separate sides" in SBUF — State Buffer) was cited and was right; I looked for it at the wrong place. It names VectorE's faster modes beside two inputs from SBUF, and the trace agrees there too: the cast, with one input, took 1.37 us for 0.43.

**The products of ones at zero: wrong.** The value lay between ends of -11 and +19 us; it was +10, by three pairs of kernels with and without them (10, 9.5 and 11 us). Rival 2 (the clock doesn't hold) had the mechanism, with 0.14. The row of 112 to 148 us, TensorE busy 34.11 of 36 us at a clock of 0.53 [rows 10], said so before the run, and I let a zero stand between the ends in spite of it. The rule of the Trainium skill (TensorE: Matmul & The Clock Gate, "What's actually happening") that activity releases the clock did not come true in the starts: the products ran at 0.61 us each.

**Rival 4 had the place and not the cause.** It had the small transfers late by d us each and the turns by 2d. In the second attention the turn was late by 5.7 us, but by the heads' and the spreading load and by VectorE; the store of the inverses, one of the transfers that it named, landed in 1.57 us where the sum had 2.2. It blamed pieces of 32 and 64 bytes; larger pieces gave nothing, and more engines did. That its size fits with d near 2.8 is chance. The Trainium skill (DMA: Bandwidth & Descriptors, "Why small descriptors are slow") is about sizes, and no run here shows sizes to matter. Its six shift waits "grow by d" hardly came: 0.6 us in the first attentions.

**The new waits on shift rows, +3 us: too small and in the wrong place**, 6.6 us more than before in all, 6.8 us of waits in the second attention, where I had put nothing, and 0.6 in the first.

## What to carry to other kernels

Price a DMA by its shape: how many pieces its outermost dimension has, and whether a row of the trace shows a transfer of such a shape, for a load of 128 KB took 5.5 us with two heads outermost and under 3 as one DMA for each head. Then look at what is issued behind a transfer that has few engines, for here it landed no earlier: taking the slow load out of one wait wasn't enough while the next link of the chain was queued behind it. When a chain of transfers replaces work on an engine at a turn between stages, lay out the last link's waits one by one, and give each consumer its own count, so that it doesn't wait for a load that it doesn't need. Filler products in a stretch in which TensorE is already busy are paid, 54 of them with 10 us here.

## What the runs showed of the hardware that I had not expected

- A DMA's share of the 16 engines followed the outermost count of its pattern, here the heads: 0.12 to 0.14 for two, 0.21 for four, 0.49 for eight, and 0.56 when each head had a DMA of 32 rows.
- A transfer issued behind one with few outermost pieces landed no earlier than it: an 8 KB store took 4.87 us behind a load of two heads and 1.57 alone, a dump of 256 KB 5.42 us behind the spreading load and 2.38 alone.
- Four DMAs issued in a row take 1.70 us on SyncE, two 0.77, one 0.56, so splitting a transfer costs 0.2 to 0.4 us for each further piece.
- GpSimd's additions and splits slowed not only VectorE's products of two inputs (0.69 to 1.99 us), but also its cast of one (0.43 to 1.37, and 1.65 beside splits alone).
- With TensorE kept busy through the turn's wait the granted clock stayed at 1.00 (2.4 GHz) there, while in the attentions' starts it stood at half although TensorE was busy for 98% of the time. What sets it there no run showed.
